# PixArt-style block on one core: the probability-times-value product as one 512-column product per head instead of two halves

## The reference, cut to what matters

```python
x = x + xattn_L0(layernorm(x), ctx, ctx, tau, delta)   # 2048 tokens, 1601 context rows, D = 256, 16 heads of 16
x = x + experts_L0(layernorm(x))                       # 8 experts, the best one is taken
x = x + window_xattn_L1(ctx, layernorm(x), ...)        # one masked attention, gaussian weights, tanh
x = x + slots_L1(layernorm(x))                         # 64 slots, top 8

def xattn_L0(q, k, v, tau, delta):
    scores = einsum('blhe,bshe->bhls', qh, kh) * tau + delta
    a = softmax(scale * scores, axis=-1)
    out = einsum('bhls,bshd->blhd', a, vh)              # the product that is changed
    return out @ Wo.T + bo
```

## Time and profile before

| what | value |
|---|---|
| runs | 1309.98 us median of 3 (1303.62 to 1311.98) |
| span of the profiled execution | 1308.7 us, mean granted TensorE clock 0.880 |
| TensorE busy | 1125.7 us, 86% |
| VectorE busy | 845.1 us, 65% |
| ScalarE busy | 547.4 us, 42% |
| GpSimd busy | 61.2 us, 5% |
| score products (L924) | 832, 408 ns mean |
| maximum units (L692) | 1102, 370 ns mean |
| probability-times-value (L768) | 3328 trace instructions, 413 ns mean, 282.2 us busy |

### The profile page before, as it was taken

One profiled execution on the slowest core, in us unless ns is written; L12 is line 12 of the kernel. 1 busy time (PEld: TensorE's weight loads), 2 busy tenths in 40 slices (PEclk: granted clock), 3 DMA queues, 4 the chain that ended last, 5 costly groups with the idle time before them and its releaser, 6 DMA issues.

```text
span 1308.7 us, 20515 instructions
## 1 busy us (share of the span) xinstructions
PE 1125.7 (86%) x6620; PEld 464.7 (36%) x6620; DVE 845.1 (65%) x1835; ACT 547.4 (42%) x1012; POOL 61.2 (5%) x75
## 2 busy tenths in 40 slices
PE   6458999999999998888999989889999888877556
PEld 3332233323433344332433343323433343344324
DVE  4547887878776775676677765667667756634232
ACT  4021266656544444554443454554444436400220
POOL 3200000000100000001000000001000000010000
PEclk9776699989989999898899887989999889978675
DMA  8995000000100000001000000010000000100231
GB/s 236 141 112 178 0 14 1 14 13 1 30 14 1 14 1 2 14 1 48 1 13 1 14 1 14 1 48 1 14 1 14 1 13 1 37 8 1 94 85 64
DMA packets 44537, 41.21 MB, mean 31 GB/s; under 512 B 10365, under 2 KB 42590, under 8 KB 44170
## 3 DMA queue, kind: packets, MB, share of 16 engines
q1 hardware_dynamic: 41850, 38.17, 12.6%
q10 hardware_dynamic: 2496, 1.35, 0.7%
q0 software_dynamic: 80, 0.26, 0.1%
HBM read 29.53 MB, written 10.59 MB: 31 GB/s over the span
## 4 chain that ended last, share of the span: by engine, by line
PE 59%; DVE 15%; issue 13%; DMA 6%; SPq 3%; DVEq 2%; ACT 1%; ACTq 0%; POOL 0%; POOLq 0%
PE ps_o L768 17%; PE ps_m L692 15%; PE ps_e L924 11%; DVE mx L1082 9%; PE ps_m L807 6%; DMA k_parts<-alphaT 2%; DMA k_stack<-q_stack 1%; DMA q_stack<-mrow 1%; PE ps_x L787 1%; SPq L381 1%; PE ps_m L993 1%; SPq L333 1%; PE ps_m L860 1%; PE ps_m L879 1%; PE ps_m L820 1%
## 5 line engine op out<-in xcount | busy, mean ns | idle before, releaser
L1082 DVE TENSOR_REDUCE mx<-ps_m 128x1 f32<-128x401 f32 x1102 | 586.8, 570 | 263.4 <-PE ps_m L692 260.6
L586 ACT ACTIVATE probs<-ps_e 128x512 f32<-128x512 f32 (+1 forms) x832 | 458.6, 596 | 523.4 <-PE ps_e L924 521.9
L692 PE MATMUL ps_m<-k_stack,q_stack 99*128 99x401 bf16 x1102 | 404.5, 370 | 60.8 <-DVE mx L1082 52.9
L924 PE MATMUL ps_e<-q_stack,k_stack 101*128 101x512 bf16 (+1 forms) x832 | 339.6, 408 | 11.4 <-issue 8.7
L768 PE MATMUL ps_o<-probs,v_heads 128*32 128x256 f32 (+1 forms) x3328 | 282.2, 413 | 0.0
L692 PEld LDWEIGHTS ps_m<-k_stack,q_stack 99*128 99x128 bf16 x1102 | 110.0, 100 | 305.4 <-DVE mx L1082 261.9
L924 PEld LDWEIGHTS ps_e<-q_stack,k_stack 101*128 101x128 bf16 (+1 forms) x832 | 86.4, 104 | 157.7 <-ACT probs L586 66.4
L807 PE MATMUL ps_m<-expert_w,xnT 128*128 128x512 f32 x256 | 120.9, 603 | 4.5 <-DVE xb L1150 3.0
L768 PEld LDWEIGHTS ps_o<-probs,v_heads 128*32 128x32 f32 (+1 forms) x3328 | 67.3, 111 | 160.8 <-issue 135.2
L1150 DVE SCALAR_TENSOR_TENSOR xb<-ps_m,hot,xb 128x256 f32<-128x256 f32 x112 | 54.2, 484 | 17.5 <-PE ps_m L807 8.1
L807 PEld LDWEIGHTS ps_m<-expert_w,xnT 128*128 128x128 f32 x256 | 47.3, 193 | 46.7 <-issue 35.8
(11 more groups left out here) (217 smaller groups left out, 676.2 us busy)
## 6 DMA issues: line engine op xcount, KB each, us to landing
q_stack<-q_parts SPq DMA_DIRECT2D x114, 64.0 KB, 2.2
k_stack<-k_parts SPq DMA_DIRECT2D x18, 256.0 KB, 14.2
q_parts<-attn_chunk SPq DMA_DIRECT2D x6, 384.0 KB, 6.0
expert_w<-in_expert_wT SPq DMA_DIRECT2D x2, 1024.0 KB, 5.8
xres<-in_x SPq DMA_DIRECT2D x4, 512.0 KB, 3.5
x<-xres SPq DMA_DIRECT2D x4, 512.0 KB, 3.7
probs<-x SPq DMA_DIRECT2D x1, 2048.0 KB, 11.0
out<-probs SPq DMA_DIRECT2D x4, 512.0 KB, 2.9
```

What stands on the lines that cost most here:

```text
L586: act.activation(probs[0:n, k % 2, h, :], ps_e[h % 2][0:n, :], ACT.Exp).then_inc(s["exp_done"], 1)
L692: pe.matmul(ps_m[:, u % 2 if banks == 2 else (UNITS * n1 + u) % banks, 0:SPLIT], qst[0:MAX_ROW, g, h, P * t:P * t + P], kst[0:MAX_ROW, HG ...
L924: pe.matmul(ps_e[h % 2][0:n, :], kst[0:ROWS, HG * g + h, P * st:P * st + n], qst[0:ROWS, g, h, :], start=True, stop=True).then_inc(s["qk_r ...
L1082: dve.tensor_reduce(mx[:, q, col:col + 1], ps_m[:, bank_of, 0:SPLIT], AX.X, ALU.max)\
```

## The change

`pv` loses its argument `half`. Instead of a product of 256 columns per head between the second and the third score product, and the other 256 columns after the fourth, it issues one product of 512 columns per head, between the second and the third. The maximum units of the slot are placed anew: in a slot with five, the third one stands in front of `pv`, and the last two behind the third and the fourth score product; before, one stood behind each score product and the fifth behind the second half.

```diff
-            def pv(c, k, half):
-                cols = slice(CT // 2 * half, CT // 2 * (half + 1))
+            def pv(c, k):
                 g, st = k // ST % NG, k % ST
                 n = rows_of(st)
...
                 for h in range(HG):
-                    mm = pe.matmul(ps_o[32 * h:32 * h + 32, cols], v_sb[0:n, st, HG * g + h, :],
-                                   probs[0:n, k % 2, h, cols], start=(st == 0 and half == 0),
-                                   stop=(st == ST - 1 and half == 1))
-                if half == 1:
-                    mm.then_inc(s["pv_done"], 1)
+                    mm = pe.matmul(ps_o[32 * h:32 * h + 32, :], v_sb[0:n, st, HG * g + h, :], probs[0:n, k % 2, h, :],
+                                   start=(st == 0), stop=(st == ST - 1))
+                mm.then_inc(s["pv_done"], 1)
...
                         if h == 2:
                             if not first:
                                 behind(c - 1, k - SHIFT)
+                            for j, u in units[2:-2]:
+                                max_unit(u, c, j)
                             if k or not first:
-                                pv(c, k - 1, 0)
+                                pv(c, k - 1)
                         need(pe, s["exp_done"], HG * SLOTS * c + HG * k + h - 1)
...
-                        for j, u in units[h:h + 1]:
+                        at_h = h if h < 2 else len(units) + h - HG
+                        for j, u in units[at_h:at_h + 1]:
                             max_unit(u, c, j)
-                    if k or not first:
-                        pv(c, k - 1, 1)
-                    for j, u in units[HG:]:
-                        max_unit(u, c, j)
```

More of the change, by code:

```diff
@@ L756, in _ @@
             pe.wait_ge(s["ld_expert"], 32)
-            def pv(c, k, half):
-                cols = slice(CT // 2 * half, CT // 2 * (half + 1))
+            def pv(c, k):
                 g, st = k // ST % NG, k % ST
                 n = rows_of(st)
[L763 to L766, removed]
+                if st == 0:
+                    need(pe, s["o_taken"], NG * c + g)
+                pe.wait_ge(s["exp_done"], HG * (SLOTS * c + k + 1))
                 for h in range(HG):
-                    mm = pe.matmul(ps_o[32 * h:32 * h + 32, cols], v_sb[0:n, st, HG * g + h, :],
-                                   probs[0:n, k % 2, h, cols], start=(st == 0 and half == 0),
-                                   stop=(st == ST - 1 and half == 1))
-                if half == 1:
-                    mm.then_inc(s["pv_done"], 1)
+                    mm = pe.matmul(ps_o[32 * h:32 * h + 32, :], v_sb[0:n, st, HG * g + h, :], probs[0:n, k % 2, h, :],
+                                   start=(st == 0), stop=(st == ST - 1))
+                mm.then_inc(s["pv_done"], 1)
             def z_columns(c, g):
@@ L941, in _ @@
                 chunk(c, False)
-            for half in range(2):
-                pv(NC, -1, half)
+            pv(NC, -1)
             z_columns(NC, -1)
```

## The result

The changed kernel takes 1374.97 us (median of four, 1369.45 to 1378.73) where the kernel before takes 1307.2: a ratio of 1.0525, interval 1.0491 to 1.0559. The forecast was 1365 us, range 1324 to 1400.

What follows compares the result with a forecast made beforehand. TensorE sets the pace, with VectorE and ScalarE close behind. 31.9 - 7.2 + 27 - 12 + 15 = +54.7 us on the 1308.7 us span gave 1363.4, so about 1365 us, range 1324 to 1400.

Steps and rivals of the forecast that it cites:

- -12 and +15 for the clock: Chunk loop: some 21 slots at 1.2 GHz gain, -12 us; 36 us more at that level behind longer stops, +15 us.
- parts 1 and 2: Plain slot: one PV group fewer saves 0.24 us, PV takes 1.00; moved waits still make it 3.59 against 3.32.
- One sign of the list: Before score products: idle time put down to ScalarE, at 0.7 us before the change, would appear.
- part 3: 118 slots without TensorE work of `behind` lose 0.27 each, +31.9 us; the other 90 gain 0.08 each, -7.2 us.
- part 4: 30 long stops for VectorE in chunks 1 to 3: next s2 0.9 us later each, +27 us (0 to 53).
- part 5: Granted clock over the chunks: -12 us and +15 us, a microsecond at the lower level costing 0.41 us.
- TensorE alone decides: Rival, whole chunk loop: waits for exponentials and reductions stay hidden, 0.24 us per slot saved, 1260 us; chance 0.06.
- the clock falls in plain slots: Rival: a third of the 118 plain slots run at the lower level, 67 us more, 1432 us; chance 0.08.
- it cancels: Rival: VectorE's queue absorbs long stops, plain slots lose 0.13 not 0.27, the clock only gains; about 1306 us; chance 0.06.

Runs made afterwards that it cites:

- The second: The changed kernel with PV split again into two halves of 256 columns, one behind the other in the same place: 1373.16 us, ratio 1.0502 to the kernel before.
- the last experiment: Third unit behind PV, `behind` after the slot's last score and units; against that kernel, PV as two adjacent 256-column products per head: 1269.87 us.
- The fifth experiment: The kernel with the third unit behind PV, but that unit ahead of PV again in 36 of 208 slots, where VectorE has long work: 1338.16 us.
- the third: The changed kernel with four banks instead of two for the maximum units in chunk 0 alone: 1348.03 us, ratio 1.031 to the kernel before.
- fourth experiments: The changed kernel with four banks for the scores in chunk 0 alone, units keeping two: 1369.92 us, ratio 1.0521 to the kernel before.

## Why the prediction was right

The forecast was +54.7 us on the span; it grew by 68.3 (1308.7 to 1377.0). Read from the third score of one slot to that of the next, the chunk loop grew by 68.3 as well (985.2 to 1053.5). By class, beside the prediction's terms (its -12 and +15 for the clock are put to the stops, since almost all of the additional time at the lower level lies there):

| steps from third score to third score | grew by, us | forecast, us |
|---|---|---|
| chunk 0 (52) | 11.6 | 14.0 |
| chunks 1 to 3, no TensorE work behind, no long stop (35) | 11.8 | 9.5 |
| chunks 1 to 3, no TensorE work behind, long stop (30: positions 7, 8, 28, 29, 32, 33, 37, 38, 42, 43) | 48.2 | 8.1 + 27 - 12 + 15 = 38 |
| chunks 1 to 3, TensorE work behind (90) | -3.4 | -7.2 |

*The block and the edges (parts 1 and 2).* PV at 1.00 and the plain slot at 3.58 were right to 0.01, and so was each wait in it. One reading was off: I gave the 0.24 us saved to merging two products into one. The second and the last experiment show that two products side by side save the same. The Trainium skill's rule, page "TensorEngine Tiling (Array Packing)", section "Key Properties", that changing the tiling mode drains TensorE, agrees with that: the cost is there at 1.00 either way, once per group. One sign of the list stood on the wrong row: idle time before scores was to grow from 0.7 us, and that row did not move. The waits are at the weight loads, 66.4 to 143.4.

*Where it holds (part 3).* The first two classes grew by 23.4 in 87 slots, 0.27 each, as forecast. This mean is in part a balance. The 47 slots of chunk 0 that are at the full clock in both traces lost 14.7, 0.31 each, since the slots with `spread_z`, left out of the forecast as covering a wait, lost 0.40 to 1.18, and two at each end of a group of heads 0.64 to 0.70; against that, chunk 0 had 12 us at the lower level before and 5 after. The covered slots gained half of what was forecast: with two expert products 0.08, as worked out, but positions 31 and 35 lost 0.5 each time.

*The long stops and the clock (parts 4 and 5).* Here the forecast was too low, 38 for 48.2, and two of its terms were off in opposite directions, so that the sum came out better than its parts. The fifth experiment moves the unit in the same 30 slots (and in six others) and gives 44 in them, so the cause is shown: the unit ahead of PV where VectorE is late. What it does not show is the split. By the clock records these 30 slots have 49 us more at the lower level than before, 20 us at 0.41. The 28 that are left are 0.9 a slot, but 0.27 of it is the plain price that part 3 counts, so the stops by themselves are 20, not 27: the 4.86 of part 4 holds a plain slot of 3.59, whose 0.27 part 3 has already. The clock then cost some 20, where part 5 had 15 - 12 = 3. Little of the gain of 12 can have come: a changed plain slot at the lower level takes 5.45 (627.36 to 632.81 us), not 5.31, and most of the time at that level lies in slots with a stop. The price of 0.41 is taken over from part 5, and no run changes the clock alone, so the two shares are argued, not shown.

*The rivals.* That TensorE alone decides would have needed banks back in time; the third and fourth experiments show the units' bank to be the one that binds. That the clock falls in plain slots is out: it stays at 1.00 from 155 to 380 us in the trace after, with TensorE waiting 0.73 of every 3.58 us. That it cancels is out as well, with 0.27 lost per plain slot and not 0.13.

*What the prediction did not see* is that the loss hung on one instruction's place. With the third unit behind PV instead of ahead of it, the same product makes the kernel 1.3% faster than before, though most of the 0.24 saved per slot still goes into waits (3.30 against 3.32) and most of the 1.3% may be the clock's. With the work behind moved to the new gap as well it is 3.1%.

## What to carry to other kernels

Before work is put together on the engine that sets the pace, ask what the pieces stood in front of: each was the cover for a bank on its way back. Follow one period through by start times, with the time after which each double-buffered bank returns; here that gave every wait of the plain slot to 0.01 us. Then fill the gaps with what does not wait: a product that needs a bank goes behind the long block, not in front of it, and independent work goes where the cover went missing.

## What the runs showed of the hardware that was not expected

Eight instructions of 512 columns and sixteen of 256, in four column groups, take the same 1.00 us from start to next start; a group of 256 alone takes 0.57. So 0.14 on leaving and 0.10 on entering (0.27 instead of 0.17 behind a unit) are paid per stay in the column groups, whether the stay has eight instructions or sixteen. It is the column groups and not fp32 as such: the expert products, fp32 over the whole array, start 0.17 behind a unit (769.62 to 769.79), and four of them bring TensorE to the next unit in 1.72, 0.43 each. And at the lower clock level the same block takes 1.87 (778.86 to 780.73).
